# A transformer block on one core: the first stack of k loaded from ScalarE's queue, the constant rows written before the columns arrive, the first maxima set among the second chunk's projections

## The reference, cut to what matters

```python
Xn = (X - mu) * rsqrt(var + EPS) * ln_g + ln_b
Q, K, V = split_heads(Xn @ Wq + bq), split_heads(Xn @ Wk + bk), split_heads(Xn @ Wv + bv)
scores = where(causal, Q @ K.T / sqrt(16), -inf)
x = layernorm(X + softmax(scores) @ V (heads joined) @ Wo + bo)
h = relu(x @ W1 + b1);  alpha = softmax(h @ W2 + b2)
x = layernorm(x + sum_k alpha_k * U_k (V_k x))
```

## Time and profile before

| what | us |
|---|---|
| runs | 467.86, 464.68, 467.00; median 467.0 |
| profiled execution | 466.19, its span 464.3 |
| busy in the span | PE 418.5, DVE 310.2, ACT 234.3, POOL 73.3 |

### The profile page before, as it was taken

The page is one execution under the profiler, slowest core; times in us unless marked ns, Lnnn a source line. Parts: engine busy times, 40 slices in busy tenths (PEclk is TensorE's granted clock), DMA queues, the critical chain, the costliest instruction groups (busy, mean ns, idle before and its releaser), DMA issues.

```text
span 464.3 us, 7228 instructions
## 1 busy us (share of the span) xinstructions
PE 418.5 (90%) x2541; PEld 209.1 (45%) x2541; DVE 310.2 (67%) x805; ACT 234.3 (50%) x498; POOL 73.3 (16%) x108
## 2 busy tenths in 40 slices
PE   7898896998999989998899987998999989997892
PEld 3355342343344433466457733434334434356452
DVE  5427995888898694326666898688889661126076
ACT  6562553675667575442441453665776665530210
POOL 2132120143021010101130022024021010100000
PEclk9899898999999999999999999899999999999797
DMA  5056662260402000001763135053220000000011
GB/s 182 0 82 96 171 97 39 32 97 12 70 1 93 2 1 0 1 2 43 129 121 48 47 54 87 0 82 59 36 35 3 1 1 2 0 0 1 0 46 45
DMA packets 18435, 21.13 MB, mean 46 GB/s; under 512 B 4960, under 2 KB 11872, under 8 KB 18400
## 3 DMA queue, kind: packets, MB, share of 16 engines
q1 hardware_dynamic: 18349, 20.66, 23.6%
q10 hardware_dynamic: 51, 0.01, 0.0%
HBM read 5.79 MB, written 2.10 MB: 17 GB/s over the span
## 4 chain that ended last, share of the span: by engine, by line
PE 64%; DVE 19%; ACT 7%; SPq 4%; issue 3%; DMA 3%; POOL 1%; DVEq 0%; ACTq 0%
PE ps L766 23%; PE ps L868 13%; PE ps L848 12%; DVE mx L656 9%; PE ps L827 9%; PE ps L831 2%; ACT pr L559 2%; DMA stq<-mrow 2%; PE ps L760 2%; SPq L448 2%; SPq L449 2%; ACT stk L517 2%; DVE st L609 2%; DVE x L616 1%; PE ps L878 1%
## 5 line engine op out<-in xcount | busy, mean ns | idle before, releaser
L559 ACT ACTIVATE pr<-ps 128x512 f32<-128x512 f32 (+3 forms) x384 | 167.3, 495 | 111.3 <-PE ps L848 109.5
L656 DVE TENSOR_REDUCE mx<-ps 128x1 f32<-128x512 f32 (+3 forms) x304 | 182.1, 653 | 34.3 <-PE ps L831 25.5
L848 PE MATMUL ps<-stq,stk 99*128 99x512 bf16 (+3 forms) x384 | 118.5, 336 | 13.8 <-DMA stq<-mrow 8.7
L827 PE MATMUL ps<-stk,stq 96*128 96x512 bf16 (+3 forms) x384 | 115.4, 332 | 2.8 <-DVE mx L656 1.7
L868 PE MATMUL ps<-pr,va 128*32 128x512 f32 (+3 forms) x768 | 82.3, 501 | 0.0
L507 POOL TENSOR_SCALAR_AFFINE_SELECT pr<-pr 128x512 f32<-128x512 f32 x64 | 40.7, 636 | 261.0 <-ACT pr L559 261.0
L848 PEld LDWEIGHTS ps<-stq,stk 99*128 99x128 bf16 x384 | 35.0, 99 | 101.5 <-ACT pr L559 51.6
L831 PE MATMUL ps<-mask,ident_b 128*128 128x128 bf16 x256 | 50.3, 223 | 0.0
L827 PEld LDWEIGHTS ps<-stk,stq 96*128 96x128 bf16 x384 | 38.0, 99 | 21.1 <-issue 6.9
L766 PE MATMUL ps<-pr,w_qk 128*128 128x512 f32 x64 | 30.7, 625 | 2.3 <-ACT pr L526 2.3
L831 PEld LDWEIGHTS ps<-mask,ident_b 128*128 128x128 bf16 x256 | 25.6, 100 | 13.0 <-issue 3.9
(11 more groups left out here) (80 smaller groups left out, 346.7 us busy)
## 6 DMA issues: line engine op xcount, KB each, us to landing
stq<-qk_raw SPq DMA_DIRECT2D x32, 96.0 KB, 2.8
stk<-qk_raw SPq DMA_DIRECT2D x32, 96.0 KB, 2.8
x_in<-in_x SPq DMA_DIRECT2D x8, 256.0 KB, 3.6
stq<-qk_raw SPq DMA_DIRECT2D x32, 64.0 KB, 2.4
stk<-qk_raw SPq DMA_DIRECT2D x32, 64.0 KB, 2.4
out_y<-x SPq DMA_DIRECT2D x3, 512.0 KB, 3.0
stk<-qk_raw SPq DMA_DIRECT2D x32, 32.0 KB, 2.4
stq<-qk_raw SPq DMA_DIRECT2D x32, 32.0 KB, 2.2
```

Of the source, the lines that this page charges most:

```text
L559: nc.scalar.activation(probs(b, g, s)[:, j, q0 - c * CHUNK:], act_bank(ev)[:, q0 - c * CHUNK:], ACT.Exp, scale=DH ** -0.5).then_inc(s_act_ ...
L656: nc.vector.tensor_reduce(dst, src, AX.X, ALU.max).then_inc(s_dve_free, 1)
L827: last = nc.tensor.matmul(bank[:, i * w:(i + 1) * w], q[0:ROWS, t // TPC, j, tile(t % TPC)], k[0:ROWS, k0 // CHUNK, j, 0:w], start=True, s ...
L848: nc.tensor.matmul(bank[:, q0 - c * CHUNK:], stk[stack_of(b, g)][0:ROWS + PARTS, kt // TPC, j, tile(kt % TPC)], stq[stack_of(b, g)][0:ROWS ...
```

## The change

Three edits, all at work in batch 0 alone.

1. ACT at its start: the one-number Exp reads `minus` (a constant that POOL has written) and no longer `cols`. The wait for `cols` now stands behind the four constant writes.
2. Stack loads of group 0 of batch 0, both chunks: the k half of each (6 of 12 transfers) is issued by ACT, at the place of the "stack" event in ACT's stream. SP keeps the 6 of q.
3. `program_order`: the second chunk's four projections were followed by the 11 maxima of group 0, with the third value pair among them. Now two projections come first, the other two stand among the 11 maxima, and the third and fourth value pair come behind "split", among the maxima of group 1.

```diff
         if b == 0:
             at_split = opening.index(("split", 0, 0, 0))
-            order += qks + woven(opening[:at_split], vs[0][2:3]) + [opening[at_split]] + vs[0][3:] + opening[at_split + 1:]
+            order += qks[:2] + woven(qks[2:4], opening[:at_split]) + qks[4:] + [opening[at_split]]
+            order += woven(vs[0][2:], opening[at_split + 1:])
...
+        def k_rows(b, g, c, i, n):
+            row = (5 * DH, 3 * DH, 0)[n]
+            parts_ = parts(1, c)[(2 * g + i) * DH:(2 * g + i + 1) * DH].rearrange("p n m s -> p n (m s)")[:, 0:n + 1]
+            return stk[stack_of(b, g)][row:row + (n + 1) * DH, c, 2 * i:2 * i + 2], parts_
...
+                        for n_part_of_q in range(PARTS):
+                            sp.wait_ge(*made(b, c)[n_part_of_q])
+                            sp.dma_start(*q_rows(b, g, c, i, n_part_of_q)).then_inc(s_stack[stack_of(b, g)][c][i], 16)
+                            if n:
+                                sp.dma_start(*k_rows(b, g, c, i, n_part_of_q)).then_inc(s_stack[stack_of(b, g)][c][i], 16)
...
         def _(act):
-            act.wait_ge(s_cols, 16)
-
-            nc.scalar.activation(le[:, 0, 0, 0:1], cols[:, 0, 0:1], ACT.Exp)
             act.wait_ge(s_one_minus, 1)
+
+            nc.scalar.activation(le[:, 0, 0, 0:1], minus[:, 0:1], ACT.Exp)
             for i in range(STACKS):
                 nc.scalar.activation(stk[i][ROWS:ROWS + PARTS].rearrange("p c h s -> p (c h s)").bitcast(F32),
                                      minus[ROWS:ROWS + PARTS, :].bitcast(F32).to_broadcast([PARTS, C * HPG * CHUNK // 2]),
                                      ACT.Copy).then_inc(s_minus, 1)
+            act.wait_ge(s_cols, 16)
...
+                if kind == "stack" and b == 0 and ev[2] == 0:
+                    _, _, g, c = ev
+                    for i in range(2):
+                        for n in range(PARTS):
+                            act.wait_ge(*made(b, c)[n])
+                            act.dma_start(*k_rows(b, g, c, i, n)).then_inc(s_stack[stack_of(b, g)][c][i], 16)
```

More of the change, by code:

```diff
@@ L381, in parts, with made, q_rows @@
             return qk_raw[:, w, c].bitcast(BF16).rearrange("p (n m s) -> p n m s", n=PARTS, m=KC)
+        def made(b, c):
+            return ((s_high, n_high["qk", b, KC - 1, c, 1]), (s_mid, n_part["part", b, KC - 1, c, 1]),
+                    (s_low, n_part["part", b, KC - 1, c, 1]))
+        def q_rows(b, g, c, i, n):
+            row, terms = (0, 3 * DH, 5 * DH)[n], PARTS - n
+            part_ = parts(0, c)[(2 * g + i) * DH:(2 * g + i + 1) * DH].rearrange("p n m s -> p n (m s)")[:, n:n + 1]
+            return (stq[stack_of(b, g)][row:row + terms * DH, c, 2 * i:2 * i + 2],
+                    part_.to_broadcast([DH, terms, KC * CHUNK]))
+        def k_rows(b, g, c, i, n):
+            row = (5 * DH, 3 * DH, 0)[n]
+            parts_ = parts(1, c)[(2 * g + i) * DH:(2 * g + i + 1) * DH].rearrange("p n m s -> p n (m s)")[:, 0:n + 1]
+            return stk[stack_of(b, g)][row:row + (n + 1) * DH, c, 2 * i:2 * i + 2], parts_
         def stack_of(b, g):
@@ L433, in _ @@
                         sp.wait_ge(s_value, n_value["value", *divmod(n - STACKS, G), ST - 1])
-                    q, k = stq[stack_of(b, g)], stk[stack_of(b, g)]
                     for i in range(2):
[L436 to L449, removed]
+                        for n_part_of_q in range(PARTS):
[3 more added lines that the diff above has]
+                                sp.dma_start(*k_rows(b, g, c, i, n_part_of_q)).then_inc(s_stack[stack_of(b, g)][c][i], 16)
                     if n == 0 and c == C - 1:
```

## The result

The changed kernel took 472.13 us (median of 4 runs, 471.46 to 474.52), the kernel before, on the same chip, 465.84 (4 runs, 464.10 to 467.86). The ratio is 1.0143, with a 95% interval of 1.0083 to 1.0203: slower, by 0.8% to 2.0%. The profiled execution took 471.91 us, with a span of 470.2; before it was 466.19 and 464.3. So there are 5.9 us of span to place.

What follows compares the result with a forecast made beforehand. PE is busiest on average, but the chain to the first score was taken to decide, with later work hanging on it. 466.19 + 6.2 (first score later) - 0.6 (low clock behind it gone) = 471.8 us; range 465.5 to 477.

Steps and rivals of the forecast that it cites:

- The head start: First four projections end at 19.3 instead of 23.3, as constants come earlier and the low clock goes: 4.0 us ahead.
- The issues on ACT: Six k issues at 0.85 us each, from 21.5 to 26.6, ahead of the turned second chunk's eviction, ending at 27.3.
- The rival of dear issues: ACT alternates with SP at 1.27 us an issue, giving 475.2; at 1.51, 478.1; chance 0.16.
- The shared block: Skill's rule: descriptor generator locked during an issue, so an ACT issue equals two of SP's; the row says 0.64 to 1.13.
- PE's gap and the clock: PE idles 5.4 us before the second value pair, which starts at 27.4, not 26.23; low clock behind charged 1.8.
- The weave: Projections among the maxima: DVE idles 1.6 + 1.5 us, turned maxima start at 46.25 instead of 44.30.
- 2.6 + 3.6 + 1.8: PE from 46.25 to first score at 54.2: turned maxima and group 1 maxima 2.6, two value pairs 3.6, low clock 1.8.
- SP's shorter queue: SP's queue is shorter by 12 x 0.64 us, worth nothing since SP waits for the rows at 55.22 anyhow.
- My second way to the score: By the rows' transfer: second six ACT issues end at 49.4, then 3.15 to the score, 52.6; PE's way is later.
- the rival where the clock holds: No clock loss after either PE gap: PE's way 50.6, transfer's 50.8, total 469.0; chance 0.19.
- What came back: Behind the first score, the low clock of 49.0 to 52.3 and DVE's idle time there go: -0.6 us.
- The rival on the other side: Not slower: the 4.0 us lead reaches the first score, at 47.4, total 465.5; chance 0.15, 0.09 for the full gain.

Runs made afterwards that it cites:

- run 1: Kernel before with only the constants moved ahead of the wait for `cols` on ACT: ratio 0.9938 (0.9897 to 0.9979).
- run 8: Kernel before with constants first; first, all twelve q and k loads of the second chunk (group 0, batch 0) on ACT: ratio 1.0039 (1.0020 to 1.0058).
- run 4: Changed kernel with 23 unread filler turns on PE ahead of the second value pair and 14 ahead of the turned maxima: ratio 1.0137 (1.0072 to 1.0203).
- run 3: Changed kernel with the old program order, so constants first and k of both chunks on ACT, no weave: ratio 1.0154 (1.0107 to 1.0201).
- run 7: Kernel before with constants first and k of the first chunk alone on ACT, old order; repeated after a useless profile: ratio 1.0140 (1.0102 to 1.0178).
- run 5: Changed kernel with the old order, and SP's five weight loads waiting for the first maxima's rows to land: ratio 1.0089 (1.0068 to 1.0109).
- run 6: Changed kernel with PE fillers in both gaps and the weight loads behind the first maxima's rows: ratio 1.0125 (1.0092 to 1.0159).
- run 2: Changed kernel with all k loads back on SP, so constants first and the weave: ratio 0.9995 (0.9964 to 1.0027).
- the last kernel of 8: Kernel before with constants first, k of the second chunk alone on ACT, weight loads behind the maxima's rows: ratio 0.9933 (0.9904 to 0.9961).
- run 9: Two kernels, constants first on the kernel before: weights behind the rows, ratio 0.9965; or five filler turns before the first score, ratio 0.9926.
- run 9's first kernel: Kernel before with constants first and the weight loads waiting for the first maxima's rows to land: ratio 0.9965 (0.9936 to 0.9994).

## Why the prediction was right, step by step

**Edit 1.** Constants at 9.62 (forecast 9.6), projections at 12.46 for 7.10 (12.3, 7.03), four projections ended at about 19.4 (19.3). The head start is 3.7 and not 4.0 us. Run 1 shows that 3.4 of it would have reached the end.

**The issues on ACT: the end right, its parts not.** I had six times 0.85, 5.1 us, from 21.5 to 26.6. The chain of the changed kernel in order of time (start us, us, what) reads otherwise:

```profile
20.89 2.28 POOL qk_raw L510 x2
23.17 0.02 issue
23.19 0.59 ACTq L551
23.77 0.04 issue
23.81 0.83 ACTq L551
24.69 0.89 ACTq L551
25.62 1.06 ACTq L551
26.73 0.79 ACT pr L538
```

The first two (0.67 and 0.62) begin at 21.12, beside the last middle part and not behind it, and are done by 22.5. The third waits for POOL's last low part until 23.17, which I had put at 22.9 and then not charged, and only four issues lie behind it. The six take 4.66 us, 0.78 each; 0.74 is that wait, the rest small gaps: 5.56. A start 0.4 too late, a price a little too high (0.82 with its gap) and a wait left out cancel to 26.68 for 26.6: luck, in this term. Without the change the eviction stands at 21.68 (run 1), with it at 26.73: 1.5 of these 5.05 us are the time to the end of the wait, 3.5 the four issues. The rival of dear issues (1.27 to 1.51) is out: the longest of the twelve took 1.06. The 1.51 that I had read belongs to the rows' transfer, which took ACT 1.32 to 1.57 us in every run, and not to ACT.

**The shared block.** SP's issues beside ACT's last three started every 0.64 to 0.82 us (24.46, 25.10, 25.92), against 0.64 when alone, and ACT's last three took 0.83 to 1.06, the three before 0.59 to 0.67. The one place before had not shown that. But it is much less than taking strict turns would cost (1.27), and that it comes from both engines issuing without a pause is not shown: in run 8 both did so from 32.99 to 35.66, ACT's took 0.59 to 0.71 and SP's still started every 0.64. Long single issues also stand where ACT issues nothing: 1.49 us at 39.03 on SP in the kernel before. What makes them long stays open. The rule of the Trainium skill that I weighed ("Perfetto Trace Analysis", DMA Instruction, HWDGE), an exclusive lock, would have given the upper price as I worked it out; the trace lies nearer the lower.

**PE's gap and the clock.** Second value pair 27.56 (27.4), gap 5.39 (5.4), its extra at the low clock 3.67 - 1.99 = 1.7 (1.8), projections ended 34.67 (34.5). Run 4 makes the idle time a shown cause of this low stretch; that an idle time need not bring one, its own 1.51 us before the score shows.

**The weave.** Third projection 36.23 (36.0), fourth 40.98 (40.45), last residual's end 44.47 (43.7), turned maxima 47.07 (46.25). DVE in that stretch:

```profile
39.64 2.94 DVE L675 TENSOR_REDUCE mx<-ps 128x1 f32<-128x512 f32 x5
43.72 0.75 DVE L659 SCALAR_TENSOR_TENSOR res<-ps,cols,qk_raw 128x512 f32<-128x512 f32 x1 [1.14 <-ACT qk_raw L564]
44.38 1.74 DVE L675 TENSOR_REDUCE mx<-ps 128x1 f32<-128x384 f32 x3
```

The term that was too small is the projection on its own: I took 1.75, a quarter of a dense row of 16, but ACT starts on its result 2.02 us after its start (36.23 to 38.25, 40.98 to 43.00). Twice that difference and the later start give the 0.8. From there to the score I had 2.6 + 3.6 + 1.8 = 8.0; it was 7.28. Run 4 splits this: with the clock held PE was ready 5.7 us behind the turned maxima (45.35 to 51.07), where I had 2.6 + 3.6 = 6.2, so the low clock cost 1.6 and not 1.8. The two errors, 0.8 too little and 0.7 too much, cancel: 54.35 for 54.2. This agreement to 0.15 us is luck.

**What I missed.** I wrote that SP's shorter queue was worth nothing since it waits at 55.22 anyhow. That looked at SP's next wait and not at what it issues before it. The weights move ahead of the rows' transfer and slow it: 6.0 us instead of 3.15 in run 3, 4.0 to 4.75 in runs 4, 7 and 8 (run 5 shows the cause; for the others it is inferred from the order of issues). My second way to the score, "3.15 from issue", 52.6, was therefore too early. In the changed kernel the rows are issued at 49.95, beside the weights (49.12 on). PE had no idle time before the score, so they had landed by 54.35; with run 4's 4.4 us, an estimate, it was just then. The two ways end nearly together, so a cure of one alone does not help fully: fillers won 1.8 of 3.3 us (run 4; both cures, run 6, 3.0), and the weave, which costs 3.3 us in run 2, adds nothing on top of run 3 (54.67 without it, 54.35 with it). The weights behind the rows alone, in the changed kernel, was not run. Had PE been sooner, as in the rival where the clock holds, the score would have stood at 52.6 (run 4) and not at 50.8.

**What came back.** DVE's 0.6 us behind the score: the distance to the second chunk's is 27.41 us, before 27.98. The sum had this term, the list of signs beside it said that the distance stays 28 us; the sum was right. Nothing else: 6.3 - 0.6, and 0.2 of small differences later, make the span's 5.9.

**The rival on the other side** asked whether the head start can reach the first score: with edit 1 alone it does. What decided against it is ACT's queue at 21.1 to 26.7, where an eviction on PE's path stands behind a wait for POOL and four issues.

## What to carry to other kernels

A queue of issues is moved for nothing or for all, by what stands behind it on that engine: six of them moved the first score by 7.5 us (43.69 in the last kernel of 8 to 51.17 in run 5, which differ in these six alone; weights held back in both) ahead of an eviction that TensorE waits for, and six like them by nothing where the eviction has time (43.80 to 43.69). A wait inside the queue counts as well: 1.5 us of it here. Whether the first six would be free if they were issued behind that eviction, no run tried. When a queue is made shorter, look at what comes next in it: bulk loads that were safely behind a small, urgent transfer may now run ahead of it; one wait on the small transfer's landing puts them back (3.5 us, run 5), and does nothing where they are behind already (run 9). And test the parts of a change by themselves: here a gain of 0.6% was buried under two losses.

## What the runs showed that I had not expected

- Weights of 1.5 MB issued ahead stretch a 12 KB transfer to 4.0 to 6.0 us from issue to score. Without them it took 2.5 to 3.2: 2.5, 3.1 and 2.5 with the weights held back (run 5, run 6, last of 8), 3.15 in the kernel before, 3.2 in run 1, 2.75 and 2.9 in run 9.
- Some executions are about 5 us longer for no reason in the edits (run 6's profiled one and likely two more of its ten, the profiled one of 12 in run 9's first kernel, likely two of four in run 4). The windows of that execution in run 9 and, below, of run 8's last kernel show the place:

```profile
220.00:250.00 30.00, 28.83 (x111) 16.30 (x111) 17.57 (x47) 9.20 (x16) 5.64 (x5) 0.89 0.58 94
250.00:285.00 35.00, 33.35 (x211) 19.79 (x210) 29.33 (x75) 14.81 (x34) 4.05 (x7) 0.95 0.30 53
```

```profile
220.00:250.00 30.00, 29.13 (x143) 18.29 (x142) 19.32 (x48) 8.85 (x16) 4.58 (x4) 1.00 0.55 91
250.00:285.00 35.00, 30.66 (x214) 16.89 (x212) 31.03 (x78) 14.48 (x36) 6.45 (x10) 1.00 0.36 62
```

  The granted clock is 0.89 and 0.95 where the other has 1.00. By that, 30 x 0.11 + 35 x 0.05 = 5.1 us should be missing, an estimate; measured between the same two scores as in run 6, it is 185.0 us against 180.2 in run 1 and in the last of 8: 4.8. It shows in the stretch between the attention of the two batches, where PE waits 1.42 us on VectorE in both. Why the clock falls there in one execution and not in the next stays open; it is a main reason why differences under 0.5% are out of reach in these comparisons.
